# Moving the work between the stages of a graph-layer megakernel: who normalises, who zeroes, and where constants and first indices are loaded

## The chip, the cores and the metric

One core of one Trainium2 chip runs the whole program in one launch. The metric is the device time of that launch in microseconds (us), as the median of several runs. The core has five engines with a queue of instructions each: TensorE (PE; PEld is its weight load), VectorE (DVE), ScalarE (ACT), GpSimd (POOL) and SyncE (SP). ACTq, SPq and so on are an engine's queue when it only issues a transfer. Engines wait for each other by semaphores, and a code block ends with a barrier of all engines.

## The reference

The input `x` has 12500 rows of 256. There are 212500 edges, sorted by destination.

```python
xn = _layernorm(x)
x = x + gnn(xn, src, dst, edge_weight) + mix(xn)   # two GCN layers; linear attention and an MLP
x = x + ffn(_layernorm(x))                          # 8 experts, one per row
# a GCN layer:
support = x @ W
msgs = support[edge_src] * edge_weight[:, None]
agg = segment_sum(msgs, edge_dst, num_segments=N)
h = elu(agg + b)
```

What matters here is the row norm at the start, and the two GCN layers, each of which reads 212500 rows by index and adds them up by destination.

## The kernel before

The program has six stages, each a block of its own between barriers: `prepare`, `gather` for layer 1, a small block `kv`, `gather` for layer 2, routing and scattering, and the experts. The change touches the first four.

**Prepare** (from L110). It normalises `x` into the scratch tensor `xn`. One step takes a block of 256 rows (128 partitions, `PB` = 2 rows each, 256 KB); 52 blocks pass through `PSLOTS` = 4 slots. SP loads a slot as soon as its last use is normalised; VectorE takes the statistics (`bn_stats`, `bn_aggr`, L273 and L277); ScalarE the root of the variance (L211); VectorE the reciprocal (L282) and the normalisation itself (L288, two instructions of 256 columns); ScalarE's queue stores the slot (L204). VectorE runs one slot ahead: statistics of slot s, then the rest of slot s-1. Before its first block VectorE reduces the destinations of the edges to windows (L254 to L267), GpSimd sends the result through memory and back (L237 to L246), and after the last block VectorE makes the tables of relative destinations (L307 to L333). SP then loads eleven constants (L197: weights and biases of later stages, and the edge weights `wgt`), and VectorE scales three of them (L335 to L337). The block ends when all of it is done.

**Gather** (from L342), once per layer. The edges go in 104 turns of 2048. In a turn GpSimd issues 16 indirect DMAs (L451), each of which fetches 128 rows by index, into one of two buffers (u = 0 and 1). VectorE builds 16 selection matrices `sel` from destinations and weights (`take`, L460 to L403), TensorE multiplies rows by selections into `sums` (L395), and VectorE adds four windows into the table `agg` (L409). Beside that each turn carries a tile of other work: keys and values of the attention in layer 1 (`keys_values`), the attention with its MLP in layer 2 (`attend`, from L1019 on VectorE), and the dense product of an earlier tile (`dense_first`, `dense_second`).

The order of the work around the change is that of the code: each engine runs its own list, and waits where a semaphore is named. GpSimd begins a turn when the turn's indices have landed (`idx_loaded`) and when TensorE has started its products on the other buffer (`rows_used`). TensorE gives buffer 0 free at its start and buffer 1 with its first product, so in each layer GpSimd can issue 16 DMAs ahead of TensorE and no more. A turn's products also wait for the windows of the turn before (`turn_added`). At the head of each gather VectorE zeroes `agg` (128 x 25216, L467), then runs `dve_begin` of the two other parts, then `take(0, 0)`. SP loads the first two turns' indices at the head of each gather (L415). Block `kv` (L821 to L830) copies the sums of layer 1's attention out of PSUM after the first gather.

Of the kernel before, what the change touches and what calls it, by code (L numbers as in the profile page):

```python
# [5 lines left out]
F32 = mybir.dt.float32  # L6
I32 = mybir.dt.int32
# [39 lines left out]
PSLOTS = 4  # L47
# [11 lines left out]
assert 1 << LOG_WIN == WIN and 1 << LOG_TB == TB and NP >= N and TURNS % 2 == 0 and NT % (PB * PSLOTS) == 0  # L59
# [50 lines left out]
def prepare(nc, m):  # L110

    with ExitStack() as ctx:
        def sb(name, shape, dt):
# [9 lines left out]
        rstd = sb("ln_rstd", [P, PSLOTS, PB], F32)  # L123
        dst_rows = sb("dst_rows", [TURNS, TURN, GROUP * P], I32)
# [18 lines left out]
        consts_loaded = sem("consts_loaded")  # L143
# [8 lines left out]
        step = sem("prepare_step")  # L152
        spans_done = sem("spans_done")
# [9 lines left out]
        x_blocks = m.x.rearrange("(b p j) f -> b p j f", p=P, j=PB)  # L163
        xn_blocks = m.xn[0:NP, :].rearrange("(b p j) f -> b p j f", p=P, j=PB)
        n_blocks = NT // PB
        loops = n_blocks // PSLOTS
        consts = [
            (m.w_q[:, :, :], m.in_w_q.rearrange("(k p) n -> p k n", p=P)),
            (m.w_m[:, :, :], m.in_w_m.rearrange("(k p) n -> p k n", p=P)),
            (m.w_1[:, :, :], m.in_w_1.rearrange("(k p) n -> p k n", p=P)),  # L170
            (m.w_2[:, :, :], m.in_w_2.rearrange("(k p) n -> p k n", p=P)),
            (m.ln1_gh[:, :], m.in_ln1_g),
            (m.ln1_b[:, :], m.in_ln1_b),
            (m.ln2_gh[:, :], m.in_ln2_g.rearrange("(o n) -> o n", o=1).to_broadcast([P, D])),
            (m.ln2_b[:, :], m.in_ln2_b.rearrange("(o n) -> o n", o=1).to_broadcast([P, D])),
            (m.gate_w[:, :, :], m.in_gate_w.rearrange("(k p) n -> p k n", p=P)),
            (m.gate_b[:, :], m.in_gate_b.rearrange("(o n) -> o n", o=1).to_broadcast([P, NE])),
            (m.wgt[:, 0:NCH], m.in_wgt),
        ]

        with nc.Block("prepare") as block:
            @block.sync
            def _(sp):
# [12 lines left out]
                for to, of in consts:  # L196
                    sp.dma_start(to, of).then_inc(consts_loaded, 16)  # L197
                sp.wait_ge(consts_loaded, 16 * len(consts))

            @block.scalar  # L200
            def _(act):
                def store(i, s):
# [4 lines left out]
                act.wait_ge(eps_set, 1)  # L207
                with act.Fori(0, loops) as i:
                    for s in range(PSLOTS):
# [3 lines left out]
                        if s:  # L213
                            store(i, s - 1)
                    store(i, PSLOTS - 1)
                act.wait_ge(zero_set, 1)

                act.dma_start(m.xn[NP:NP + P, :], m.zeros[:, 0:D]).then_inc(pad_stored, 16)
# [5 lines left out]
            def _(pool):  # L224
                nc.gpsimd.memset(m.zeros[:, :], 0.0).then_inc(zero_set, 1)
# [21 lines left out]
                             m.more_dram.rearrange("(o t) g -> o t g", o=1)).then_inc(spans_back, 16)  # L247

            @block.vector
            def _(dve):  # L250
                nc.vector.memset(m.eps[:, :], LN_EPS).then_inc(eps_set, 1)
                dve.wait_ge(edges_loaded, 32)
# [15 lines left out]
                stat_steps = 7  # L268

                def statistics(i, s):  # L270
                    dve.wait_ge(x_loaded[s], 16 * i + 16)
                    for j in range(PB):
                        last = nc.vector.bn_stats(stats[:, s, j, :], rows[:, s, j, :])  # L273
                    last.then_inc(step, 1)
                    wait_apart(dve, step, i * PSLOTS + (s + stat_steps), m.passed)
                    for j in range(PB):
                        last = nc.vector.bn_aggr(mv[:, s, j, :], stats[:, s, j, :])  # L277
                    last.then_inc(mv_done, 1)

                def normalise(i, s, first):  # L280
                    dve.wait_ge(sd_done, i * PSLOTS + (s + 1))
                    nc.vector.reciprocal(rstd[:, s, :], sd[:, s, :]).then_inc(rstd_done, 1)  # L282
                    dve.wait_ge(rstd_done, i * PSLOTS + (s + 1))
                    if not first:

                        dve.wait_ge(xn_stored[s], 16 * i)
                    for j in range(PB):
                        last = nc.vector.tensor_scalar(normed[:, s, j, :], rows[:, s, j, :], mv[:, s, j, 0:1],  # L288
                                                       rstd[:, s, j:j + 1], ALU.subtract, ALU.mult)
                    last.then_inc(xn_done, 1)  # L290

                def turn(i, first):

                    for s in range(PSLOTS):
                        statistics(i, s)
                        if s:
                            normalise(i, s - 1, first)
                        elif not first:
                            normalise(i - 1, PSLOTS - 1, isinstance(i, int) and i == 1)
# [1702 lines left out]
```

## Time and profile before

| | |
|---|---|
| median of 3 runs | 5263.27 us (5253.92 to 5268.12) |
| the profiled execution | 5257.51 us |
| its span | 5255.6 us |
| mean granted TensorE clock | 0.85 of 2.4 GHz |
| PE, DVE, ACT, POOL busy | 4074.3, 2650.4, 814.5, 3445.0 us |

The span runs from the first to the last instruction of the profiled execution; 1.9 us of its time lie outside. The stages take about 148 us (prepare), 2126 us (first gather with `kv`), 2150 us (second gather) and 830 us (the rest). A busy time on GpSimd here is the making of a DMA's descriptors.

### The profile page before, as it was taken

What the parts mean: (1) busy time and instruction counts of PE and PEld (TensorE: products, weight loads), DVE (VectorE), ACT (ScalarE), POOL (GpSimd) and SP (SyncE); (2) the same over time, 40 slices, a digit from 0 to 9 for tenths busy, and PEclk for the clock granted to TensorE, in tenths of its full rate; (3) what the DMA queues carried; (4) which work ended last, traced back from release to release, by engine and by line L of the source; (5) the groups of instructions that cost most, each with busy time, mean ns of one, the idle gap of its engine ahead of it and who ended that gap; (6) DMA issues with size and microseconds to landing.
All of it is one profiled execution on the core that took longest, in us unless ns stands there. A gap on an engine that the chain in (4) does not pass through costs nothing. (4 is left out here: it accounts for less than half of the span.)

```text
span 5255.6 us, 89454 instructions
## 1 busy us (share of the span) xinstructions
PE 4074.3 (78%) x25266; PEld 3747.3 (71%) x25267; DVE 2650.4 (50%) x9578; ACT 814.5 (15%) x2507; POOL 3445.0 (66%) x3639
## 2 busy tenths in 40 slices
PE   0577777777777777769988999898989987069998
PEld 0467666666667776758888888888888886058886
DVE  7433333333333333355676666767666666234444
ACT  2001111111111111111222222222222222011111
POOL 0577777777777777757777777777777774632222
PEclk9867777777777777778999999999999998589999
DMA  7444444444444444434555454555545553632221
GB/s 212 142 128 132 130 132 132 130 132 130 132 131 133 132 130 132 129 89 125 147 147 152 143 151 145 147 149 146 151 144 148 147 146 109 188 112 70 67 70 65
DMA packets 409075, 693.81 MB, mean 132 GB/s; under 512 B 108237, under 2 KB 275661, under 8 KB 408893
## 3 DMA queue, kind: packets, MB, share of 16 engines
q0 software_dynamic: 177312, 488.43, 32.8%
q1 hardware_dynamic: 195765, 163.17, 10.6%
q10 hardware_dynamic: 35920, 41.25, 2.2%
q8 instruction: 40, 0.66, 0.0%
q14 instruction: 38, 0.31, 0.0%
HBM read 562.84 MB, written 129.68 MB: 132 GB/s over the span
## 5 line engine op out<-in xcount | busy, mean ns | idle before, releaser
L395 PEld LDWEIGHTS sums<-sel,rows 128*128 128x128 f32 x13312 | 1888.7, 222 | 768.0 <-DMA rows<-xn,idx 440.8
L395 PE MATMUL sums<-sel,rows 128*128 128x64 f32 x13312 | 1894.5, 305 | 672.9 <-DMA rows<-xn,idx 354.6
L451 POOL DMA_INDIRECT rows<-xn,idx x1664 | 1577.8, 948 | 642.4 <-issue 630.8
L451 POOL DMA_INDIRECT rows<-h,idx x1664 | 1585.3, 953 | 578.5 <-issue 528.9
L403 DVE TENSOR_SCALAR sel<-cols,rel_now,wgt_now 128x64 f32<-128x64 f32 x3360 | 780.4, 336 | 7.8
L409 DVE TENSOR_TENSOR agg<-agg,sums 128x128 f32 x832 | 240.3, 289 | 783.9 <-issue 604.7
L603 DVE TENSOR_TENSOR pre<-z,b_g 128x256 f32<-128x256 f32 x98 | 41.6, 424 | 526.8 <-PE z L598 526.8
L1807 PE MATMUL y_ps<-w,e_hidden 128*128 128x256 f32 x1248 | 286.1, 389 | 0.0
L1795 PE MATMUL e_hidden_ps<-tokens_t,w 128*128 128x256 f32 x1248 | 279.2, 381 | 4.4 <-DVE e_hidden L1864 3.6
L983 PE MATMUL hidden_ps<-xt,w 128*128 128x128 f32 x1664 | 265.2, 282 | 17.2 <-ACT msg_t L1104 17.0
L1735 POOL DMA_INDIRECT out<-y_result,target_i x80 | 79.5, 994 | 291.3 <-DVE y_result L1849 271.3
L1795 PEld LDWEIGHTS e_hidden_ps<-tokens_t,w 128*128 128x128 f32 x1248 | 237.5, 191 | 40.0 <-DVE e_hidden L1864 6.6
L1807 PEld LDWEIGHTS y_ps<-w,e_hidden 128*128 128x128 f32 x1248 | 241.8, 196 | 33.3
L983 PE MATMUL hidden_ps<-msg_t,w 128*128 128x128 f32 x1664 | 254.2, 275 | 0.0
L983 PEld LDWEIGHTS hidden_ps<-xt,w 128*128 128x128 f32 x1664 | 221.3, 193 | 35.3 <-ACT msg_t L1104 35.3
L946 PE MATMUL row_ps<-w,hidden 128*128 128x256 f32 x832 | 223.6, 418 | 2.7 <-ACT hidden L1108 2.7
L983 PEld LDWEIGHTS hidden_ps<-msg_t,w 128*128 128x128 f32 x1664 | 219.7, 192 | 0.0
L779 PE MATMUL kv_proj<-w_k,kv_xt 128*128 128x256 f32 x416 | 210.0, 660 | 0.0
L795 DVE TENSOR_SCALAR k_min<-kv_proj 128x256 f32<-128x256 f32 x104 | 44.1, 424 | 302.3 <-PE kv_proj L779 302.3
L946 PEld LDWEIGHTS row_ps<-w,hidden 128*128 128x128 f32 x832 | 170.1, 215 | 26.1 <-ACT hidden L1108 2.9
L971 PE MATMUL row_ps<-w_m,msg_t 128*128 128x256 f32 x416 | 125.4, 426 | 71.2 <-ACT msg_t L1096 71.2
L779 PE MATMUL kv_proj<-w_v,kv_xt 128*128 128x256 f32 x416 | 174.8, 567 | 0.0
(211 smaller groups left out, 4547.4 us busy)
## 6 DMA issues: line engine op xcount, KB each, us to landing
xe<-zeros ACTq DMA_DIRECT2D x104, 258.0 KB, 4.1
rows<-xn,idx POOLq DMA_INDIRECT x1664
rows<-h,idx POOLq DMA_INDIRECT x1664
w<-in_ffn_w POOLq DMA_DIRECT2D x16, 1024.0 KB
tile<-xn SPq DMA_DIRECT2D x105, 128.0 KB
ln_rows<-in_x SPq DMA_DIRECT2D x52, 256.0 KB
xn<-ln_normed ACTq DMA_DIRECT2D x52, 256.0 KB, 4.4
kv_tile<-xn SPq DMA_DIRECT2D x104, 128.0 KB
```

The lines of the kernel that those rows point to most:

```text
L395: last = nc.tensor.matmul(sums[:, g, h, :], rows[:, u, k, h * P:(h + 1) * P], sel[:, u, k, :], start=(c == 0), stop=(c == GROUP - 1))
L403: last = nc.vector.tensor_scalar(sel[:, u, k, :], m.cols[:, :], rel_now[:, u, k:k + 1], wgt_now[:, u, k:k + 1], ALU.is_equal, ALU.mult)
L409: return nc.vector.tensor_tensor(window, window, sums[:, g, :, :], ALU.add)
L451: nc.gpsimd.indirect_dma_start(out=rows[:, u, k, :], out_offset=None, in_=source, in_offset=bass.IndirectOffsetOnAxis(ap=idx[:, u, k:k + 1 ...
L779: last = nc.tensor.matmul(proj[n][:, 0, :], xt[:, k, :], w[:, k, :], start=(k == 0), stop=(k == KD - 1))
L795: nc.vector.tensor_scalar(k_min[:, :], proj[0][:, 0, :], 0.0, None, ALU.min).then_inc(k_min_ready, 1)
L946: last = nc.tensor.matmul(row_ps[1], hidden[:, o, :], m.w_2[:, o, :], start=(o == 0), stop=(o == F1 // P - 1))
L971: last = nc.tensor.matmul(row_ps[0], msg_t[:, k, :], m.w_m[:, k, :], start=(k == 0), stop=(k == KD - 1))
L983: last = nc.tensor.matmul(hidden_ps[:, o, :], m.w_1[:, k, o * P:(o + 1) * P], of, start=(k == 0), stop=(k == 2 * KD - 1))
L1735: nc.gpsimd.indirect_dma_start(out=m.out, out_offset=bass.IndirectOffsetOnAxis(ap=target_i[:, tt:tt + 1], axis=0), in_=result[:, tt, :], i ...
L1795: last = nc.tensor.matmul(hidden_ps[f % HB], w1[u][:, k, f * P:(f + 1) * P], tokens_t[:, k, :], start=(k == 0), stop=(k == KD - 1))
L1807: last = nc.tensor.matmul(y_ps[tt], hidden[:, f, tt * P:(tt + 1) * P], w2[u][:, f, :], start=(f == 0), stop=(f == FC - 1))
```

## The change

- **The norm.** ScalarE does the normalisation, as one activation per 256 columns with the reciprocal as scale and a shift as bias; VectorE computes the shift (minus mean times reciprocal). Seven slots in place of four, 49 blocks in place of 52: the six tiles of padding past row 12543 are zeroed by one store, issued by ScalarE's queue at the start. ScalarE's table for root and identity is loaded once, ahead of the loop.
- **Edge tables.** VectorE takes the first seven blocks' statistics before the reductions over the edges, and makes the tables before the last seven blocks rather than after them.
- **Constants.** `wgt` is loaded by GpSimd's queue at the start. The ten other constants are loaded by SP at the head of the first gather, behind its own two weights and ahead of the dense part's; VectorE scales three of them at the end of the first gather.
- **Indices.** The buffer `idx` is shared by both gathers. SP loads the first two turns' indices at the end of prepare for the first gather, and at the end of the first gather for the second. GpSimd's first two turns are written out ahead of its loop.
- **Zeroing.** For layer 1 GpSimd zeroes `agg` in prepare, after its last transfer there. For layer 2 VectorE still does, but after `take(0, 0)`.
- **`kv`** is no block of its own; its copies stand at the end of VectorE's list in the first gather (`dve_close`).

```diff
-PSLOTS = 4
+PSLOTS = 7
...
-        n_blocks = NT // PB
+        n_blocks = UNITS // PB
...
-                for to, of in consts:
-                    sp.dma_start(to, of).then_inc(consts_loaded, 16)
-                sp.wait_ge(consts_loaded, 16 * len(consts))
+                for u in range(2):
+                    sp.dma_start(m.idx[:, u, :], m.in_src[u]).then_inc(m.idx_first, 16)
+                sp.wait_ge(m.idx_first, 32)
...
+                def normalise(i, s, first):
+                    wait_apart(act, rstd_done, 2 * (i * PSLOTS + s + 1), m.act_passed)
+                    if not first:
+                        act.wait_ge(xn_stored[s], 16 * i)
+                    for j in range(PB):
+                        last = nc.scalar.activation(normed[:, s, j, :], rows[:, s, j, :], ACT.Identity,
+                                                    scale=rstd[:, s, j:j + 1], bias=shift[:, s, j:j + 1])
+                    last.then_inc(xn_done, 1)
                     act.wait_ge(xn_done, i * PSLOTS + s + 1)
...
+                act.preload_act_table_set("sqrt_and_others")
...
+                pool.dma_start(m.wgt[:, 0:NCH], m.in_wgt).then_inc(wgt_loaded, 16)
                 nc.gpsimd.memset(m.zeros[:, :], 0.0).then_inc(zero_set, 1)
...
+                nc.gpsimd.memset(m.agg[:, :, :], 0.0).then_inc(agg_zeroed, 1)
...
+                def scale(i, s):
+                    dve.wait_ge(sd_done, i * PSLOTS + (s + 1))
+                    nc.vector.reciprocal(rstd[:, s, :], sd[:, s, :]).then_inc(rstd_done, 1)
+                    dve.wait_ge(rstd_done, 2 * (i * PSLOTS + s) + 1)
+                    nc.vector.scalar_tensor_tensor(shift[:, s, :], mv[:, s, :, 0], -1.0, rstd[:, s, :],
+                                                   ALU.mult, ALU.mult).then_inc(rstd_done, 1)
...
+                turn(0, True)
                 dve.wait_ge(edges_loaded, 32)
...
-                turn(0, True)
-                turn(1, False)
-                with dve.Fori(2, loops) as i:
+                with dve.Fori(1, loops - 1) as i:
                     turn(i, False)
-                normalise(loops - 1, PSLOTS - 1, False)
...
+                turn(loops - 1, False)
+                scale(loops - 1, PSLOTS - 1)
+                wait_apart(dve, agg_zeroed, 1, m.passed)
...
                 for u in range(2):
-                    sp.dma_start(idx[:, u, :], m.in_src[u]).then_inc(idx_loaded[u], 16)
                     mix.load(sp, u, u)
                 mix.load_weights(sp)
                 dense.load_weights(sp)
...
+                if layer == 1:
+                    for u in range(2):
+                        sp.wait_ge(rows_loaded[u][BANKS - 1], 16 * GROUP * SUB * loops)
+                        sp.dma_start(idx[:, u, :], m.in_src[u]).then_inc(m.idx_first, 16)
...
+                pool.wait_ge(m.idx_first, 32 * layer)
+                turn(0)
+                wait_apart(pool, rows_used[1], 1, m.pool_passed)
+                turn(1)
+                with pool.Fori(1, loops) as i:
...
-                nc.vector.memset(m.agg[:, :, :], 0.0).then_inc(agg_zeroed, 1)
+                take(0, 0)
+                if layer == 2:
+                    nc.vector.memset(m.agg[:, :, :], 0.0).then_inc(agg_zeroed, 1)
                 mix.dve_begin(dve)
                 dense.dve_begin(dve)
-                take(0, 0)
...
+        for to, of in consts:
+            sp.dma_start(to, of).then_inc(consts_loaded, 16)
```

Three places show how the engines' lists change. The names are the program's tiles; a row is one instruction, or several of one kind.

ScalarE in prepare, one block inside the loop, before: root, then the address and the issue of the store of the slot before.

```order
L211 ACTIVATE ln_sd<-ln_mean_var,eps 128x2 [waits mean_var_done]
L204 ISA [waits xn_done]
L204 DMA xn<-ln_normed 128x512
L210 REGISTER_ALU
L211 ACTIVATE ln_sd<-ln_mean_var,eps 128x2 [waits mean_var_done]
```

The same place in the changed kernel:

```order
L206 ACTIVATE ln_sd<-ln_mean_var,eps 128x2 [waits mean_var_done]
L66 REGISTER_ALU
L194 REGISTER_ALU [waits rstd_done]
L196 ACTIVATE ln_normed<-ln_rows,ln_shift,ln_rstd 128x256 [waits xn_stored0]
L196 ACTIVATE ln_normed<-ln_rows,ln_shift,ln_rstd 128x256
L200 ISA [waits xn_done]
L200 DMA xn<-ln_normed 128x512
```

Two activations of 256 columns have moved in between the root and the store, and the store's wait is now for ScalarE's own work.

VectorE at the head of the second gather, before, from the copies of `kv` on:

```order
L830 COPY kv<-kv_total1 32x2
L821 UNCONDITIONAL_BRANCH
L456 UNCONDITIONAL_BRANCH
L467 MEMSET agg 128x25216
L1019 TENSOR_SCALAR q_min2<-tile_ps2 128x256
L1357 MEMSET logits 128x48
L460 COPY rel_now2<-dst_rel 128x16
L462 COPY wgt_now2<-wgt 128x16
L403 TENSOR_SCALAR sel2<-cols,rel_now2,wgt_now2 128x64 x16
L1041 SCALAR_TENSOR_TENSOR q_min2<-tile_ps2,q_min2 128x256
```

The same place in the changed kernel:

```order
L858 COPY kv<-kv_total1 32x2
L408 UNCONDITIONAL_BRANCH
L465 UNCONDITIONAL_BRANCH
L469 COPY rel_now2<-dst_rel 128x16
L471 COPY wgt_now2<-wgt 128x16
L400 TENSOR_SCALAR sel2<-cols,rel_now2,wgt_now2 128x64 x16
L478 MEMSET agg 128x25216
L1048 TENSOR_SCALAR q_min2<-tile_ps2 128x256
L1386 MEMSET logits 128x48
L1070 SCALAR_TENSOR_TENSOR q_min2<-tile_ps2,q_min2 128x256
```

The first selections stand ahead of the zeroing; the attention's first step (`q_min2`) still stands behind it.

GpSimd from the end of prepare into the first gather, before:

```order
L246 DMA more_row<-more_dram 1x16x13
L181 UNCONDITIONAL_BRANCH
L79 ISA
L443 UNCONDITIONAL_BRANCH
L445 UNCONDITIONAL_BRANCH
L445 ISA
L66 REGISTER_ALU
L451 DMA rows<-xn,idx 128x256 x32
```

And in the changed kernel:

```order
L250 DMA more_row<-more_dram 1x16x13
L252 MEMSET agg 128x25216
L170 UNCONDITIONAL_BRANCH
L79 ISA
L443 UNCONDITIONAL_BRANCH
L447 DMA rows<-xn,idx 128x256 x32
```

The zeroing of the table has come to GpSimd's list in prepare, and its first 32 indirect DMAs stand ahead of the loop.

## Rows read from the trace of the kernel before

**Rows 1.** The page's costliest groups, GpSimd: count | busy us, mean ns | idle before

```profile
L451 POOL DMA_INDIRECT rows<-xn,idx x1664 | 1577.8, 948 | 642.4 <-issue 630.8
L451 POOL DMA_INDIRECT rows<-h,idx x1664 | 1585.3, 953 | 578.5 <-issue 528.9
```

**Rows 2.** Timeline of the first gather: start us, us, engine, line [idle before it]

```profile
147.97 0.33 SPq L415 DMA_DIRECT2D idx<-in_src  x1
...
150.71 1.04 POOL L451 DMA_INDIRECT rows<-xn,idx  x1 [126.78 <-issue]
...
153.30 21.07 DVE L467 MEMSET agg<- 128x25216 f32 x1 [6.42 <-issue]
...
169.59 0.95 POOL L451 DMA_INDIRECT rows<-xn,idx  x1 [0.30 <-issue]
...
178.30 3.64 PE L395 MATMUL sums<-sel,rows 128*128 128x64 f32 x16 [19.42 <-DVE sel L403]
...
179.76 0.94 POOL L451 DMA_INDIRECT rows<-xn,idx  x1 [9.23 <-issue]
...
2243.12 0.95 POOL L451 DMA_INDIRECT rows<-xn,idx  x1 [0.30 <-issue]
```

**Rows 3.** Timeline of prepare: first edges, one block, tables, last wait

```profile
9.99 2.29 DVE L254 TENSOR_REDUCE low<-dst_rows 104x4 int32<-104x2048 int32 x1 [8.87 <-DMA dst_i<-in_dst]
...
16.17 0.74 DVE L273 BATCH_NORM_STATS2 ln_stats<-ln_rows 128x6 f32<-128x256 f32 x2
...
42.34 0.29 ACT L211 ACTIVATE ln_sd<-ln_mean_var,eps 128x2 f32<-128x2 f32 x1 [1.58 <-DVE ln_mean_var L277]
42.39 0.73 DVE L288 TENSOR_SCALAR ln_normed<-ln_rows,ln_mean_var,ln_rstd 128x256 f32<-128x256 f32 x2
...
43.28 0.37 ACTq L204 DMA_DIRECT2D xn<-ln_normed  x1
...
136.28 0.19 DVE L307 CAST cols<-iota_i 128x64 f32<-128x64 int32 x1
...
140.03 0.07 DVE L333 MEMSET wgt<- 128x16 f32 x1
146.31 0.17 DVE L335 TENSOR_SCALAR ln_gh<-ln_gh 128x2 f32<-128x2 f32 x1 [6.21 <-DMA wgt<-in_edge_weight]
```

**Rows 4.** Stretches of prepare: us, busy (count) by engine, PEclk, DMA share, GB/s

```profile
60.00:110.00 50.00, 0.00 (x0) 0.00 (x0) 38.33 (x154) 12.07 (x26) 0.00 (x0) 1.00 0.81 227
136.00:144.00 8.00, 0.00 (x0) 0.00 (x0) 4.01 (x16) 0.00 (x0) 0.00 (x0) 1.00 1.07 385
```

**Rows 5.** Groups by shape, ScalarE and GpSimd: count | busy us, mean ns | idle before

```profile
L1104 ACT ACTIVATE msg_t<-turn_ps,ln_b,ln_gh 128x128 f32<-128x128 f32 x208 | 84.1, 457 | 59.6 <-PE turn_ps L976 59.5
...
L1077 ACT COPY xt<-tile_ps 128x256 f32<-128x256 f32 x105 | 39.5, 376 | 3.5 <-PE tile_ps L932 3.4
...
L1819 ACT COPY tokens_t<-e_turn_ps 128x512 f32<-128x512 f32 x40 | 23.4, 586 | 241.5 <-PE e_turn_ps L1784 241.5
...
L1744 POOL MEMSET y_zeros<- 128x512 f32 x1 | 0.6, 603 | 0.0
```

**Rows 6.** Timeline between the two gathers and of the second one's start

```profile
2271.02 0.28 DVE L825 MEMSET kv<- 128x264 f32 x1 [3.90 <-PEq L411]
...
2273.74 0.36 SPq L415 DMA_DIRECT2D idx<-in_src  x1
...
2276.36 0.94 POOL L451 DMA_INDIRECT rows<-h,idx  x1 [32.30 <-DMA idx<-in_src]
...
2279.07 21.07 DVE L467 MEMSET agg<- 128x25216 f32 x1 [6.47 <-issue]
...
2300.81 3.66 DVE L403 TENSOR_SCALAR sel<-cols,rel_now,wgt_now 128x64 f32<-128x64 f32 x16
...
2306.07 0.95 POOL L451 DMA_INDIRECT rows<-h,idx  x1 [10.00 <-issue]
...
2323.84 1.90 PE L395 MATMUL sums<-sel,rows 128*128 128x64 f32 x16
```

More of the change, by code:

```diff
@@ L205, in store, with turn @@
                                   normed[:, s, :, :]).then_inc(xn_stored[s], 16)
-                act.wait_ge(eps_set, 1)
-                with act.Fori(0, loops) as i:
+                def turn(i, first):
                     for s in range(PSLOTS):
@@ L213, in _ @@
                         if s:
-                            store(i, s - 1)
-                    store(i, PSLOTS - 1)
+                            normalise(i, s - 1, first)
+                    normalise(i, PSLOTS - 1, first)
+                act.preload_act_table_set("sqrt_and_others")
                 act.wait_ge(zero_set, 1)
-                act.dma_start(m.xn[NP:NP + P, :], m.zeros[:, 0:D]).then_inc(pad_stored, 16)
+                tiles = (NP - UNITS * P) // P + 1
+                act.dma_start(m.xn[UNITS * P:NP + P, :].rearrange("(t p) f -> p t f", p=P),
+                              m.zeros[:, 0:D].rearrange("p (o f) -> p o f", o=1).to_broadcast([P, tiles, D])
+                              ).then_inc(pad_stored, 16)
+                act.wait_ge(eps_set, 1)
+                turn(0, True)
+                with act.Fori(1, loops) as i:
+                    turn(i, False)
                 act.wait_ge(pad_stored, 16)
@@ L251, in _, with statistics, turn @@
                 nc.vector.memset(m.eps[:, :], LN_EPS).then_inc(eps_set, 1)
+                def statistics(i, s):
+                    dve.wait_ge(x_loaded[s], 16 * i + 16)
+                    for j in range(PB):
+                        last = nc.vector.bn_stats(stats[:, s, j, :], rows[:, s, j, :])
+                    last.then_inc(stats_done, 1)
+                    wait_apart(dve, stats_done, i * PSLOTS + s + 1, m.passed)
+                    for j in range(PB):
+                        last = nc.vector.bn_aggr(mv[:, s, j, :], stats[:, s, j, :])
+                    last.then_inc(mv_done, 1)
+                def scale(i, s):
[4 more added lines that the diff above has]
+                                                   ALU.mult, ALU.mult).then_inc(rstd_done, 1)
+                def turn(i, first):
+                    for s in range(PSLOTS):
+                        statistics(i, s)
+                        if s:
+                            scale(i, s - 1)
+                        elif not first:
+                            scale(i - 1, PSLOTS - 1)
+                turn(0, True)
                 dve.wait_ge(edges_loaded, 32)
@@ L564, in _ @@
                 dense.pe_end(pe)
-        mix.after()
 def dense_first(nc, m, sb, sem, ps, shared):
@@ L1117, in attend @@
     mix.load_weights = lambda sp: None
-    mix.after = lambda: None
+    mix.dve_close = lambda dve: None
     return mix
```

130 lines of the change are left out of this document (56 added, 74 removed).

## The prediction

> **What bounds the kernel now.** I read the page's groups first. The two gathers issue 1664 indirect DMAs each, and GpSimd is busy 0.95 us with one [rows 1]. The timeline of the first gather then shows what stands between two of them: from the DMA at 179.76 to the last at 2243.12 there are 1647 steps in 2063.4 us, 1.253 us each, with 0.30 us of idle time at every step [rows 2]. So from its seventeenth DMA on the first gather is nothing but GpSimd's issue rate: 16 x 1.253 = 20.05 us a turn, whatever TensorE and VectorE do. The second gather has the same step (0.95 us busy each [rows 1]) with a few gaps more. A change that leaves that rate alone can gain only at the seams: the time before GpSimd's first DMA of each gather, and the time in which it stands still near the head. I looked for these next.
>
> There are four. Prepare keeps GpSimd from its first DMA until 150.71. After 16 DMAs it stands 10.17 us instead of 1.25 (169.59 to 179.76), because buffer 1 is given free by TensorE's first product, which starts at 178.30, waiting for selections that VectorE makes behind 21.07 us of zeroing [rows 2]. Between the gathers, block `kv` starts at 2271.02, the next block's first instruction is at 2273.74, and GpSimd's first DMA at 2276.36 waited for its indices [rows 6]. At the head of the second gather it stands still again, 10.00 us until 2306.07, behind the same zeroing [rows 6].
>
> Prepare itself isn't held by transfers: in its loop the DMA engines moved 227 GB/s, and 385 GB/s in the stretch behind it [rows 4]. From 16.17 to 136.28 it takes 52 blocks, 2.31 us each [rows 3]; VectorE is busy 38.33 of 50 us [rows 4], or 1.77 us a block, and waits on ScalarE for the rest.
>
> **Part 1, prepare's pace.** VectorE loses the two normalising instructions (0.73 us [rows 3]) and gains a shift of 2 columns (about 0.15, an estimate like the other tiny ones): 1.77 - 0.73 + 0.15 = 1.2 busy, with its semaphore gaps some 1.4 us a block. ScalarE gains what VectorE loses. A pair of its activations with scale and bias read per partition takes 84.1 / 104 = 0.81 us at 128 columns, and 256 columns more cost 586 - 376 = 210 ns, so 128 more cost 0.105 [rows 5]: 0.81 + 2 x 0.105 = 1.02 us for a block. Its list for a block is then the root 0.29, the pair 1.02, 0.16 from the end of normalising (42.39 + 0.73) to the store's issue at 43.28, the issue 0.37 [rows 3], and 0.1 of register work (an estimate): **1.94 us**. That is more than VectorE's 1.4 and more than the 1.4 us that 2 x 262 KB take at 385 GB/s, so ScalarE becomes prepare's bound. Bounds of its pace: 1.4 (VectorE's, if the pieces overlap), and 2.3 (two activations that don't overlap, 2 x 0.56, and 0.3 of registers).
>
> The first block. Its load stands behind the two edge loads in SP's queue, which landed at 9.99 [rows 3]; 0.26 MB more at 385 GB/s is 0.7. New in the same moments are `wgt` (0.85 MB) and the store of padding (0.92 MB), 4.6 us at that rate if all of it goes first. So the block lands between 10.7 and 15.3; I take 14, since three queues share. Its root starts 1.2 later, the second block's 1.4 behind it, and those up to the sixth at 1.94: 14 + 1.2 + 1.4 + 4 x 1.94 = 24.4. VectorE scales the sixth (0.7) and turns to the edge reductions, 16.17 - 9.99 = 6.2 us [rows 3]. ScalarE's seventh normalisation waits for them and for the statistics and scaling behind them (1.6), since VectorE runs only one block ahead: 32.9, and 1.55 for the pair and its store: 34.4. Six rounds of seven blocks follow, 6 x (7 x 1.94 + 0.3 for the branch) = 83.3: 117.7. The tables ahead of the last round take 140.10 - 136.28 = 3.8 [rows 3], of which two normalisations hide about 1.8: 119.7. The last store lands some 4 us later: 123.7. The block's closing takes 1.1 (from the end of the scalings begun at 146.31 to 147.97 [rows 2, 3]): the first gather starts at **124.8 instead of 147.97, 23.2 earlier**. The 6.21 us wait for the last constant [rows 3] is gone with it. The new loads of indices are hidden by the last stores. GpSimd's zeroing is priced at nothing because it has from about 40 us to 120 and takes between 21.07 (VectorE's time for it [rows 2]) and 25216 / 512 x 0.603 = 29.7 us [rows 5]; without that cover it would cost its length (rival B).
>
> **Part 2, the first gather's head.** GpSimd now starts 150.71 - 147.97 = 2.74 after the block [rows 2]. With its indices there this is between 0.3 (its idle time between two DMAs) and 2.74; I take 0.9, a gain of 1.8. The zeroing is off VectorE, which starts 5.33 us into the block (153.30 - 147.97 [rows 2]) and makes its selections in some 4 us. TensorE also waits for the dense part's weights, which SP now issues behind ten constants: 9 us of issue, landing near 15 us into the block (estimate; 25 at worst). GpSimd needs buffer 1 at 0.9 + 20.05 = 21: no stall, and 10.17 - 1.25 = **8.9 us** gained, 5 at worst. The 2.3 MB of constants share the DMA engines with the rows; the gather's stretch has room. Every later turn keeps its 20.05 us.
>
> **Part 3, between the gathers.** The copies of `kv` now run on VectorE while SP still waits for its last store, so the block's 2273.74 - 2271.02 = 2.7 us shrinks to a closing of 0.7: **2.0** gained (0.5 to 2.7). The three scalings join them there. SP's loads of indices now stand ahead of its last stores of `h` and wait for the last rows; those stores have some 10 us of room.
>
> **Part 4, the second gather's head.** Here the zeroing stays on VectorE, behind the selections instead of ahead of them, and the stall moves rather than goes. TensorE's first product no longer waits, so GpSimd runs 32 DMAs through, to 0.9 + 40.1 = 41 us into the block. But it then wants buffer 0, which TensorE frees with turn 1's first product, and that needs turn 0's windows, hence the attention's steps behind the zeroing. Before: zeroing ended 26.4 into the block (2279.07 + 21.07 - 2273.74), turn 1's product came 23.7 later, at 2323.84, and GpSimd began turn 2 at 2306.07 + 20.05, 52.4 into the block [rows 6]. After: VectorE's first instruction again at 5.33, selections 4.0 (3.66 and two copies [rows 6]), zeroing to 30.4. Of the 23.7, the selections' 4.0 go, and about 2 of products made earlier: 18, so 48.4. GpSimd follows 1.46 behind the product (179.76 - 178.30 [rows 2]): turn 2 at 49.9, **2.5** sooner than 52.4, with a new wait of some 9 us at the thirty-third DMA. Bounds: 0 (nothing of the 23.7 goes but what the later zeroing takes) to 11.4 (no stall, 41).
>
> **Sum.** 23.2 + 1.8 + 8.9 + 2.0 + 2.5 = 38.4. Everything behind the second gather's head is shifted, not changed. Against the profiled execution's 5257.5 that gives 5219.1. The median of the three runs lies 5.8 above that execution, the mean of all four 3.2; I put the forecast at **5220**.
>
> **Rivals.**
> - **B, GpSimd's zeroing holds VectorE up.** Both write the same memory, and if one of the loop's VectorE instructions can't run beside the long GpSimd one, VectorE stops for up to 21 to 30 us, and ScalarE one block later: about 22 lost, **5242**. For it: no row shows a long GpSimd instruction beside VectorE's loop. Against: the selections run beside GpSimd's issues in 3.66 us [rows 6]. The Trainium skill, SBUF — State Buffer, section Who interferes with whom, says that a GpSimd instruction holds a port pair it shares with VectorE for its whole length, and that VectorE's copies, casts and tensor_scalars stop for it, others with two SBUF inputs only if GpSimd reads. By that the statistics and the shift run on, while the reciprocal is in neither list; no run here shows it.
> - **C, the second head's stall goes altogether.** VectorE's first instruction comes 5.33 us into both gathers though it waits for nothing [rows 2, 6]. If the new code takes that away, zeroing ends at 25 and turn 2 can start near 44.6: 5.3 more, **5215**; with less behind the zeroing, 5211. The Trainium skill, Runtime: NRT & Kernel Launch, section Instruction fetch mechanics, says that a branch out of the fetched window costs a fetch before the engine goes on; by that the lag depends on where the new code falls. The trace agrees in that the lag is the same twice.
> - **D, ScalarE's pieces overlap** and VectorE bounds prepare at 1.43: 48 x 0.51 = 24 more, **5195**. Against: the store's issue waits for its own normalisation.
> - **E, slower: ScalarE is too slow for the norm.** Each 0.1 us a block costs 4.8 us, so from 1.94 + 38.4 / 48 = 2.74 us a block on the change loses. At 3.3, as with one table load more a block, it gives **5284**. Against: the order shows one load ahead of the loop, and the bound from rows is 2.3.
>
> **How the numbers follow.** Forecast 0.70, B 0.08, C 0.11, D 0.08, E 0.03. The low end takes in D, 5195; the high end takes the pace of 2.3 (48 x 0.36 = 17) with the late first block, and B: 5243. A measurement of this kernel can tell about 0.3%, 15.8 us, from no change. Faster by more than that needs 23 of the 38 us to hold: 0.93. E is slower, 0.02 of it by over 0.3%; the rest is within.
>
> **What would show it.** Right: ScalarE's stores in prepare 1.9 to 2.0 us apart and no table load in the loop; GpSimd's first DMA near 126; no gap at its seventeenth DMA of either gather, and one of about 9 us at the second gather's thirty-third; 1.253 us a step in between. Wrong: stores 2.3 us or more apart; a hole in VectorE's statistics while GpSimd zeroes; a gap at the seventeenth DMA (weights behind constants); another step than 1.253, since 1% of it is 42 us in the two gathers, more than all I count.

## The result, and the profile after

The changed kernel takes 5373.92 us (median of four runs, 5364.52 to 5380.38) against 5259.25 before (5253.92 to 5268.12): a ratio of **1.0215, 95% interval 1.0193 to 1.0237**. It is slower by 2.1%, where the prediction said 5220. The profiled execution spans 5374.1 us, against 5255.6 before.

GpSimd's issues cut the span into five stretches, each of which can be set against its counterpart. These are the rows of the changed kernel's timeline for them (start us, us, engine, line [idle before it]); the rows of before are [rows 2, 6].

```profile
124.04 1.04 POOL L447 DMA_INDIRECT rows<-xn,idx  x1 [67.98 <-POOLq L80]
...
146.96 0.94 POOL L447 DMA_INDIRECT rows<-xn,idx  x1 [3.05 <-PE sums L392]
...
2214.06 0.95 POOL L447 DMA_INDIRECT rows<-xn,idx  x1 [0.30 <-issue]
...
2243.22 0.95 POOL L447 DMA_INDIRECT rows<-h,idx  x1 [28.21 <-POOLq L80]
...
2296.87 0.94 POOL L447 DMA_INDIRECT rows<-h,idx  x1 [13.89 <-PE sums L392]
...
4520.52 0.95 POOL L447 DMA_INDIRECT rows<-h,idx  x1 [0.30 <-issue]
```

Of before, one row more is needed, the last DMA of its second gather:

```profile
4406.95 0.95 POOL L451 DMA_INDIRECT rows<-h,idx  x1 [0.30 <-issue]
```

| stretch, us | before | after | difference |
|---|---|---|---|
| start to GpSimd's first DMA | 150.7 | 124.0 | -26.7 |
| first gather, first to last DMA | 2092.4 | 2090.0 | -2.4 |
| last DMA to the second gather's first | 33.2 | 29.2 | -4.1 |
| second gather, first to last DMA | 2130.6 | 2277.3 | **+146.7** |
| last DMA to the end of the span | 848.7 | 853.6 | +4.9 |

So by the second gather's first DMA the change is 33.1 us ahead, and everything is lost in that gather. GpSimd's own step is the same there (1.25 us between most of its DMAs, 0.30 idle), but from about 2600 us on it stands still in nearly every turn, for 0.8 to 5.3 us. Two of these places:

```profile
2691.04 0.94 POOL L447 DMA_INDIRECT rows<-h,idx  x1 [5.28 <-issue]
...
2755.59 0.94 POOL L447 DMA_INDIRECT rows<-h,idx  x1 [2.75 <-PE sums L392]
```

The engine that makes it wait is found in the groups of VectorE's instructions: `q_min` in line 1070 (1041 before) is the first instruction that works behind the loop's jump. First how its idle time is split in the kernel before (us, times), then in the changed one:

```profile
L1041 DVE SCALAR_TENSOR_TENSOR q_min<-tile_ps,q_min x104: 409/425/426, 2304.4 to 4405.9; 128x256 f32<-128x256 f32 x104
its engine sat idle before it (us, times) until:
  ACT q_min L1081: 49.6, 103
```

```profile
L1070 DVE SCALAR_TENSOR_TENSOR q_min<-tile_ps,q_min x104: 423/425/426, 2273.9 to 4520.8; 128x256 f32<-128x256 f32 x104
its engine sat idle before it (us, times) until:
  issue: 150.4, 45
  ACT q_min L1110: 28.5, 59
```

"issue" is idle time in which the engine waited for nothing that the profile shows. It comes 45 times, 3.3 us each. The loop has 46 rounds of two turns, so that is once at each jump back: VectorE stands still right behind it. The 150.4 us are about what the gather loses, 146.7. What moved meanwhile is in the page's section on DMA queues (packets, MB, share of 16 engines), before and after:

```profile
q14 instruction: 38, 0.31, 0.0%
```

```profile
q14 instruction: 265, 2.17, 0.1%
```

The 227 packets more are five for each of 45 jumps (225) and two besides, and 2.17 MB / 265 is 8192 bytes a packet. Their start times in the trace fit: in each of the 45 stops two of these packets begin, the first within 1.2 us of the stop's start. So at each jump back VectorE's instructions are fetched again. No instruction of the loop was changed; what changed is where it stands, because other VectorE instructions ahead of it were added.

The Trainium skill, Runtime: NRT & Kernel Launch, section Instruction fetch mechanics, says that a taken branch whose target isn't in the fetched window forces a fetch before the engine goes on. The trace agrees, at 3.3 us a time.

### The profile page after: what moved, and what is told of

It reads as the page before. It is cut to its first block and busy times, and to the rows that moved or that the text cites. A ratio compares the mean times of both kernels' runs of the same rounds, so it can differ in the third digit from the quotient of the medians.

```text
span 5374.1 us, 89394 instructions
## 1 busy us (share of the span) xinstructions
PE 4167.9 (78%) x25266; PEld 3824.0 (71%) x25267; DVE 2601.0 (48%) x9507; ACT 851.0 (16%) x2590; POOL 3472.7 (65%) x3641
## 3 DMA queue, kind: packets, MB, share of 16 engines
q14 instruction: 265, 2.17, 0.1%
## 5 line engine op out<-in xcount | busy, mean ns | idle before, releaser
L392 PEld LDWEIGHTS sums<-sel,rows 128*128 128x128 f32 x13312 | 1919.7, 225 | 743.5 <-DMA rows<-xn,idx 441.3
L392 PE MATMUL sums<-sel,rows 128*128 128x64 f32 x13312 | 1922.5, 308 | 646.8 <-DMA rows<-xn,idx 352.0
L1012 PE MATMUL hidden_ps<-xt,w 128*128 128x128 f32 x1664 | 266.7, 283 | 13.9 <-ACT msg_t L1133 13.6
L975 PE MATMUL row_ps<-w,hidden 128*128 128x256 f32 x832 | 256.8, 464 | 3.1 <-ACT hidden L1137 3.1
L975 PEld LDWEIGHTS row_ps<-w,hidden 128*128 128x128 f32 x832 | 191.3, 241 | 33.4 <-ACT hidden L1137 3.3
L1042 ACT ACTIVATE ln_var<-var 128x1 f32<-128x1 f32 x208 | 42.2, 203 | 880.7 <-DVE var L1024 880.7
L1813 PE MATMUL e_turn_ps<-ident,tokens 128*128 128x128 f32 x160 | 27.2, 298 | 189.8 <-DMA tokens<-xe 189.8
```

Source lines behind the costliest of these rows:

```text
L392: last = nc.tensor.matmul(sums[:, g, h, :], rows[:, u, k, h * P:(h + 1) * P], sel[:, u, k, :], start=(c == 0), stop=(c == GROUP - 1))
L975: last = nc.tensor.matmul(row_ps[1], hidden[:, o, :], m.w_2[:, o, :], start=(o == 0), stop=(o == F1 // P - 1))
L1012: last = nc.tensor.matmul(hidden_ps[:, o, :], m.w_1[:, k, o * P:(o + 1) * P], of, start=(k == 0), stop=(k == 2 * KD - 1))
L1042: nc.scalar.activation(ln_var[:, n, :], var[:, n, :], ACT.Ln).then_inc(log_ready[n], 1)
```

## The experiments

**The place of the loop.** Counted in the built programs, VectorE's loop of the second gather is 328 instructions long and begins at its instruction 3093 in the kernel before and 3144 in the changed one. My theory: what counts is how many pieces of 128 instructions the loop touches, one packet of 8192 bytes each. (That a packet holds 128 is at first an estimate: the same section of the Trainium skill gives 32 KiB as 512 instructions, 64 bytes each. The runs with 128 memsets below test it.) From 3093, place 21 of a piece, it ends at place 348 and touches three; from 3144, place 72, it ends at place 399 and touches four. To move it and nothing else, small memsets of a spare tile stand at VectorE's very start, in `prepare`:

```diff
                 nc.vector.memset(m.eps[:, :], LN_EPS).then_inc(eps_set, 1)
+                for k in range(77):
+                    nc.vector.memset(pad[:, k:k + 1], 0.0)
```

Four kernels, two made from the changed one and two from the kernel before:

> The changed kernel with 77 small memsets of one column each (a spare tile, never read) on VectorE at the very start of the prepare block, where VectorE otherwise waits for the first rows of x until 13.03 us (hidden: that much idle is there). They move every later VectorE instruction 77 places on, so that the loop of the second gather begins at VectorE's instruction 3221 instead of 3144, which is exactly 128 places behind its 3093 in the kernel before. Theory (place of the loop in VectorE's code): the refetch after each back-branch (44 of them at a mean of 3.46 us, 152.4 us together, against 9.2 us before) goes, the instruction packets of the queue q14 fall from 265 to some 40 to 60, and the time falls from 5374 to 5374 - 143 = 5231, with the 33.1 us that the seams gained kept: 5215 to 5235. Rival (something the edits do in the second gather itself: the sums zeroed later, the new form of the gather's loop, the early indices): no instruction of that gather changes, so 5365 to 5385 stays.

> The same with 128 small memsets. Theory (place of the loop relative to pieces of 128 instructions, 8192 bytes, the size of one packet of q14): a whole piece more leaves the loop where it stands in its pieces, so the refetches stay, 5365 to 5390, and 240 to 290 packets on q14. Rival (any shift helps, or the memsets at the start help by themselves): 5215 to 5240, as with 77.

> The kernel before, none of the edits, with 51 of the same small memsets at VectorE's start, so that its second gather's loop begins at instruction 3144, the place that it has in the changed kernel. Theory: the refetches come, some 44 x 3.2 us = 143 us and more, 5390 to 5410, and over 240 packets on q14. Rival (the edits themselves): 5250 to 5270, as the kernel before.

> The kernel before with 128 of the memsets (one whole piece of 8192 bytes). Theory: same place within its pieces, so 5255 to 5275 (VectorE has idle time at the start for most of the memsets) and about 38 packets on q14. Rival (more code ahead of the loop is what costs, wherever it then stands): 5350 or more.

And four that put the ends of the loop near a piece's edge, with one run each:

> The changed kernel with 64 of the small memsets. The second gather's loop is 328 VectorE instructions long; with 64 it runs from instruction 3208 to 3535, which is places 8 to 335 counted from a multiple of 128, within three pieces of 128. Theory (no refetch while the loop lies within three pieces): 5210 to 5240, 38 to 60 packets on q14. Rival (only the very place of the kernel before is good): 5360 to 5390.

> The changed kernel with 48 of the small memsets: the loop runs from 3192, place 120 of a piece, to 3519, so that its first 8 instructions lie in a fourth piece. Theory: the refetches are back, 5360 to 5390 and 240 packets or more on q14, although only 16 memsets fewer than with 64 stand ahead. Rival (pieces begin elsewhere than at the multiples of 128 that I count, or a loop that overhangs by a few instructions is spared): 5210 to 5240.

> The kernel before with 28 of the small memsets: its loop runs from 3121, place 49, to place 376, within three pieces (384). Theory: as the kernel before, 5245 to 5270, some 38 packets on q14. Rival (every shift of the kernel before costs): 5390 or more.

> The kernel before with 44 of the small memsets: its loop runs from place 65 to place 392, so its last 9 instructions, the back-branch among them, lie in a fourth piece. Theory: refetches, 5390 to 5420, 240 packets or more on q14. Rival (the pieces end later): 5245 to 5270.

Measured:

| kernel | memsets | loop's places | pieces | packets on q14 | us | ratio to before, 95% |
|---|---|---|---|---|---|---|
| before | 0 | 21 to 348 | 3 | 38 | 5259 | |
| b_pad28 | 28 | 49 to 376 | 3 | 38 | 5261.1 (one run) | |
| b_pad44 | 44 | 65 to 392 | 4 | 264 | 5413.2 (one run) | |
| b_pad51 | 51 | 72 to 399 | 4 | 264 | 5410.4 | 1.0283 (1.0266 to 1.0301) |
| b_pad128 | 128 | 21 to 348 | 3 | 39 | 5257.5 | 1.000 (0.999 to 1.001) |
| changed | 0 | 72 to 399 | 4 | 265 | 5373.9 | 1.0215 (1.0193 to 1.0237) |
| a_pad48 | 48 | 120 to 447 | 4 | 265 | 5496.8 (one run) | |
| a_pad64 | 64 | 8 to 335 | 3 | 40 | 5233.9 (one run) | |
| a_pad77 | 77 | 21 to 348 | 3 | 40 | **5223.1** | 0.9936 (0.9919 to 0.9954) |
| a_pad128 | 128 | 72 to 399 | 4 | 266 | 5372.4 | 1.0214 (1.0197 to 1.0231) |

All eight came out on the theory's side, and none as its rivals would have it. The kernel before, with none of the edits, is 2.8% slower when its loop stands where the changed kernel's does (b_pad51), and the changed kernel is 0.64% faster than before when its loop stands where the old one did (a_pad77). That it isn't the number of instructions ahead is told by the two with 128: a whole piece more changes nothing, in either kernel. The idle rows of `q_min` go the same way, here in a_pad77 and then in b_pad51:

```profile
  ACT q_min L1113: 50.1, 104
```

```profile
  issue: 150.1, 45
  ACT q_min L1084: 28.0, 58
```

Two pairs of neighbours tell where a piece begins: 64 memsets are fast, 48 are not, and 28 are fast ahead of the old loop and 44 are not. The fast places seen are 8, 21 and 49, the slow ones 65, 72 and 120, and of 128 places the 57 from 0 to 56 should be fast. What the engine holds beyond that isn't measured.

a_pad48 had been expected at 5360 to 5390 and took 5497: the direction held, the size didn't. Its packets are as many, but VectorE stands still at a second place in the round as well. These are its groups for `q_min` and for `rel_now`, the copy right behind it (count | busy us, mean ns | idle before):

```profile
L1073 DVE SCALAR_TENSOR_TENSOR q_min<-tile_ps,q_min 128x256 f32<-128x256 f32 x104 | 44.2, 425 | 156.7 <-issue 128.2 <-ACT q_min L1113 28.5
...
L472 DVE COPY rel_now<-dst_rel 128x16 f32 (+1 forms) x210 | 39.3, 187 | 121.4 <-issue 92.6 <-DMA b_g<-in_gnn_b 15.9 <-PEq L80 6.9
```

In the changed kernel that copy had 28.8 us of idle time and none of it by "issue". The two rows by "issue" make 220.8 of the 274 us between this run and a_pad77. So the place of the loop among the pieces changes the price too, not only whether it is paid; which instructions stand at the edges may be the reason, but that wasn't followed up.

**ScalarE normalises.** With the loop at a good place, the parts can be told apart. The first is the largest term of the prediction.

```diff
-                    wait_apart(act, rstd_done, 2 * (i * PSLOTS + s + 1), m.act_passed)
...
-                        last = nc.scalar.activation(normed[:, s, j, :], rows[:, s, j, :], ACT.Identity,
-                                                    scale=rstd[:, s, j:j + 1], bias=shift[:, s, j:j + 1])
...
                     nc.vector.reciprocal(rstd[:, s, :], sd[:, s, :]).then_inc(rstd_done, 1)
...
+                        last = nc.vector.tensor_scalar(normed[:, s, j, :], rows[:, s, j, :], mv[:, s, j, 0:1],
+                                                       rstd[:, s, j:j + 1], ALU.subtract, ALU.mult)
```

> One part undone: VectorE normalises again (root on ScalarE, reciprocal and the two subtract-and-scale instructions on VectorE, ScalarE only issues the store), all else as in the changed kernel, seven slots and edge tables beside the rows included. The second round of prepare is written out, so 114 small memsets stand ahead instead of 77, which puts the second gather's loop at instruction 3349, again place 21 of a piece. Theory (the prediction's part 1): a block goes back from some 1.92 us to some 2.3, over 42 to 48 blocks 16 to 18 us: GpSimd's first DMA near 141 instead of 124.6, and 5237 to 5243 against 5223. Rival (the seven slots and the rows that start earlier gain it, ScalarE is not needed): GpSimd's first DMA at 126 or before and 5218 to 5228.

Measured: 5241.75 us, ratio 0.9965 (0.9952 to 0.9979), GpSimd's first DMA at 143.09. The numbers are the theory's, and the theory is wrong all the same. The timeline of VectorE and GpSimd in `prepare` (one pair a block, 0.74 us) shows where the 18 us are:

```profile
37.92 0.77 DVE L271 TENSOR_SCALAR ln_normed<-ln_rows,ln_mean_var,ln_rstd 128x256 f32<-128x256 f32 x2
...
39.83 21.42 DVE L271 TENSOR_SCALAR ln_normed<-ln_rows,ln_mean_var,ln_rstd 128x256 f32<-128x256 f32 x2
...
62.38 0.74 DVE L271 TENSOR_SCALAR ln_normed<-ln_rows,ln_mean_var,ln_rstd 128x256 f32<-128x256 f32 x2
```

```profile
39.65 21.13 POOL L246 MEMSET agg<- 128x25216 f32 x1
```

One pair took 21.42 us; it began 0.18 us behind GpSimd's zeroing and ended 0.47 behind it. Nothing else in prepare is slower. The roots on ScalarE that open a round give the pace: a round of four blocks before, then one of seven in the changed kernel, then one of seven with VectorE normalising again (a77_norm_dve).

```profile
64.36 1.28 ACT L211 ACT_TABLE_LOAD   x1 [3.35 <-DVE ln_normed L288]
65.66 0.48 ACT L211 ACTIVATE ln_sd<-ln_mean_var,eps 128x2 f32<-128x2 f32 x2
...
73.65 1.28 ACT L211 ACT_TABLE_LOAD   x1 [3.46 <-DVE ln_normed L288]
74.94 0.48 ACT L211 ACTIVATE ln_sd<-ln_mean_var,eps 128x2 f32<-128x2 f32 x2
```

```profile
76.01 0.48 ACT L206 ACTIVATE ln_sd<-ln_mean_var,eps 128x2 f32<-128x2 f32 x2 [0.94 <-ACT ln_normed L196]
...
90.35 0.48 ACT L206 ACTIVATE ln_sd<-ln_mean_var,eps 128x2 f32<-128x2 f32 x2 [0.94 <-ACT ln_normed L196]
```

```profile
83.31 0.53 ACT L200 ACTIVATE ln_sd<-ln_mean_var,eps 128x2 f32<-128x2 f32 x2 [3.36 <-DVE ln_normed L271]
...
96.84 0.53 ACT L200 ACTIVATE ln_sd<-ln_mean_var,eps 128x2 f32<-128x2 f32 x2 [3.35 <-DVE ln_normed L271]
```

That is 9.28 us for four blocks (2.32 each), 14.34 for seven (2.05) and 13.53 for seven (1.93). VectorE normalising is the faster of the two, so it isn't the engine that shortened a block. The rows of before show what did: a load of ScalarE's table stands ahead of the first root of every round, and the changed kernels load it once, ahead of their loop. This is the group of the loads in before:

```profile
L211 ACT ACT_TABLE_LOAD x13 | 16.7, 1283 | 43.3 <-DVE ln_normed L288 42.1 <-DVE eps L251 1.1
```

VectorE's reciprocal has to wait for the root behind that load. This is its idle time by it (us, times) in before (L282), then in a77_norm_dve (L266):

```profile
  ACT ln_sd L211: 12.7, 12
```

```profile
  ACT ln_sd L200: 0.2, 1
```

That is 12.7 of the 20 us or so by which 52 blocks of 2.32 differ from 52 of 1.93. The rest is left for the longer round. No run changes the load or the slots alone, so this split is read from the traces and not shown by an experiment. Taking GpSimd's zeroing away should give back the 22 us. The last experiment does that and joins it with the split below:

```diff
-                nc.gpsimd.memset(m.agg[:, :, :], 0.0).then_inc(agg_zeroed, 1)
...
+                if layer == 1:
+                    nc.scalar.activation(m.agg[:, :, :], m.zeros[:, 0:1].rearrange("p (a b) -> p a b", a=1)
+                                         .to_broadcast([P, KD, AGG]), ACT.Copy).then_inc(agg_zeroed, 1)
                 mix.act_begin(act)
```

> VectorE normalises again as in a77_norm_dve (114 memsets, the second gather's loop at place 21), and GpSimd's zeroing in prepare is taken away: ScalarE zeroes the table at the start of the first gather, and one half of it in the second (the split of a77_zero_split). In a77_norm_dve one normalising pair on VectorE took 21.42 us, ending 0.47 us behind GpSimd's zeroing of 21.13, and apart from that a round of seven blocks took 13.5 us against 14.4 with ScalarE normalising. Theory (VectorE's normalising instruction stands still while GpSimd zeroes, and that alone made ScalarE's part worth 18 us): no normalising pair over 1 us, GpSimd's first DMA at 143.1 - 22.6 + 1.9 = 122 (121 to 124), and 5208 to 5216 us, no worse than the 5213 of a77_zero_split. Rival (VectorE's pace is what holds prepare, ScalarE is needed for it): GpSimd's first DMA at 135 or later and 5222 or more.

Measured: 5211.72 us, ratio **0.9904 (0.9888 to 0.9921)**, GpSimd's first DMA at 122.19, and the pair that had taken 21.42:

```profile
39.59 0.74 DVE L269 TENSOR_SCALAR ln_normed<-ln_rows,ln_mean_var,ln_rstd 128x256 f32<-128x256 f32 x2
```

So ScalarE's part is worth nothing by its pace; beside GpSimd's zeroing it is worth 18 us, because it takes the instructions off VectorE that can't run beside it. The statistics, reciprocals and shifts of the changed kernel's loop ran beside the same 21.13 us with no such stop: the longest wait among them, 2.69 us, is for ScalarE's root. The Trainium skill, SBUF — State Buffer, section Who interferes with whom, names `tensor_scalar` among the VectorE instructions that can stop for a GpSimd instruction's whole length; the trace agrees.

**The second gather's head.**

```diff
-                take(0, 0)
                 if layer == 2:
                     nc.vector.memset(m.agg[:, :, :], 0.0).then_inc(agg_zeroed, 1)
+                take(0, 0)
```

> One part undone: in the second gather the zeroing of the sums stands ahead of the first selections again; 77 memsets, the loop at the same place as with 77. With 77 GpSimd stood 13.8 us at the thirty-third DMA and not at the seventeenth; in the kernel before 10.9 at the seventeenth. Theory from those two rows: the order of the change costs 3 us here, so 5220 against 5223, a stall of 10 to 11 us at the seventeenth DMA and none at the thirty-third. Rival (the prediction's part 4, which gave the change 2.5 us at this place): 5226, and a wait at the thirty-third DMA as well.

Measured: 5230.62 us, ratio 0.9949 (0.9934 to 0.9964), which can't be told from a_pad77's 0.9936 (0.9919 to 0.9954); the two profiled spans are 5224.8 and 5224.5. The time lies above both that were expected, 5220 and 5226. The stall is at the seventeenth DMA, and only there:

```profile
2271.45 0.94 POOL L450 DMA_INDIRECT rows<-h,idx  x1 [11.39 <-PE sums L395]
```

Whether the zeroing stands ahead of the selections or behind them moves the stall by sixteen DMAs and leaves its size within 1.5 us (12.84 behind them, in a_pad77). So neither 3 us one way nor 2.5 the other is shown.

```diff
-                    nc.vector.memset(m.agg[:, :, :], 0.0).then_inc(agg_zeroed, 1)
+                    nc.vector.memset(m.agg[:, 0, :], 0.0).then_inc(agg_zeroed, 1)
...
-                    dve.wait_ge(agg_zeroed, 1)
+                    wait_apart(dve, agg_zeroed, 2, m.passed)
...
         copy_tile(act, 0, 0)
+        nc.scalar.activation(m.agg[:, 1, :], m.zeros[:, 0:1].to_broadcast([P, AGG]), ACT.Copy
+                             ).then_inc(m.agg_zeroed, 1)
         exp_query(act, 0)
```

> With 77 memsets and, in the second gather, the zeroing split: VectorE zeroes one half of the table, ScalarE the other, between its first copy of the tile and its first exponential. Theory (the stall at the thirty-third DMA is the length of the zeroing carried through turn 0's attention): both halves are done near 2256 instead of 2269, the stall falls from 13.8 to 1 to 4 us, and the time to 5210 to 5214. It tells also what the 5.12 us of idle time are that stand ahead of the zeroing on VectorE: if they are part of the zeroing, they halve to 2.6; if they belong to the instruction, 5.1 stay and the gain is some 2 us less. Rival (the attention's chain of turn 0, not the zeroing, sets the stall; or ScalarE's half holds up its own first steps): 12 us or more of stall, 5220 to 5228.

Measured: 5212.91 us, ratio 0.9915 (0.9901 to 0.9928). GpSimd has no step over 2 us at the head of this gather any more, and the gather is 2121.4 us long instead of 2133.1 in a_pad77; the intervals of the two times overlap, the 11.7 us of the trace are what the theory said. VectorE's half:

```profile
2246.57 10.56 DVE L482 MEMSET agg<- 128x12608 f32 x1 [2.50 <-DMA b_g<-in_gnn_b]
```

## Why the prediction was wrong, point by point

**The step that failed** is the sentence in its sum, "Everything behind the second gather's head is shifted, not changed". It rests on GpSimd's issue rate as the only bound, "whatever TensorE and VectorE do", so nothing was set down for what VectorE's loop costs at its new place. But the loop's place in VectorE's code is shifted with the rest, by 51 instructions, and by that it costs 3.3 us more at each jump back. 146.7 us of loss stand against 33.1 of gain. Nor had the second gather the room that was read from the first. These are 1000 us of the first gather and 1730 of the second in the kernel before (us; busy of PE, PEld, DVE, ACT and POOL; granted clock, DMA share, GB/s):

```profile
500.00:1500.00 1000.00, 747.97 (x4098) 690.39 (x4097) 353.74 (x1349) 103.39 (x300) 756.88 (x799) 0.75 0.47 131
2650.00:4380.00 1730.00, 1553.84 (x11486) 1455.04 (x11485) 1188.15 (x4477) 390.06 (x1357) 1288.54 (x1352) 0.96 0.51 148
```

TensorE, whose products wait for VectorE in every turn, is busy for 75% of the one and 90% of the other; that this is why hardly any of VectorE's stop was hidden is argued from these rows. With the loop at its old place the same edits give 5223.1 (a_pad77), against 5220 forecast. Rival C came near the cause, since it let a fetch of code depend on where the new code falls, but only for the 5 us at a block's start.

The prediction had asked to look for another step than 1.253 us. The step itself stayed; what came was a wait in nearly every turn, from a stop of VectorE in every other.

**Prepare and the first DMA: the pace right, the reason for the gain wrong.** First DMA at 124.0, forecast some 125.7; VectorE's first block at 13.03, forecast 14; a pair of activations 1.08 us, forecast 1.02; ScalarE's stores 1.92 apart inside a round, forecast 1.94. These rows are of the changed kernel (ScalarE, two blocks):

```profile
37.52 1.08 ACT L196 ACTIVATE ln_normed<-ln_rows,ln_shift,ln_rstd 128x256 f32<-128x256 f32 x2
38.76 0.36 ACTq L200 DMA_DIRECT2D xn<-ln_normed  x1
39.24 0.29 ACT L206 ACTIVATE ln_sd<-ln_mean_var,eps 128x2 f32<-128x2 f32 x1 [0.64 <-DVE ln_mean_var L265]
39.44 1.08 ACT L196 ACTIVATE ln_normed<-ln_rows,ln_shift,ln_rstd 128x256 f32<-128x256 f32 x2
40.68 0.37 ACTq L200 DMA_DIRECT2D xn<-ln_normed  x1
```

But the gain of the loop was put down to VectorE's lighter list, from 2.31 us a block [rows 3] and 38.33 busy of 50 [rows 4]. With VectorE normalising and nothing zeroed beside it, GpSimd's first DMA comes no later (122.19, norm_dve_zero_act). Before, the seam between two rounds of four cost 9.28 - 4 x 1.88 = 1.8 us, where 1.88 is the distance of two roots within a round; with seven slots, the table loaded ahead of the loop, and VectorE normalising it costs 13.53 - 7 x 1.88 = 0.4. Of the 1.8, 1.28 is the table load. The prediction read that VectorE "waits on ScalarE for the rest", but didn't ask for what: it never costed the load that goes, nor PSLOTS going from 4 to 7. What it did cost held: three blocks fewer (3 x 2.31 = 6.9 us), the constants' wait that is gone, and ScalarE as the bound at 1.92 us a block. So its time for the first DMA was no luck; wrong is why that comes sooner than before. The table load accounts for more of it than the work that was moved, which a77_norm_dve and norm_dve_zero_act show to gain nothing by itself.

**Rival B** was false for the kernel as written, and right about the hazard: undoing ScalarE's part brought out a stop of 21.4 us, at the low end of its 21 to 30. GpSimd's zeroing itself took 21.13, within the bounds.

**The first gather's head** gained 6.2 us of stall, not 8.9: 3.05 us stay (1.35 in a_pad77, so part of it varies). It is the gap that the prediction named as a sign of weights behind constants. In the changed kernel the dense part's last weight is issued behind the ten constants, 13.6 us into the gather, and VectorE waits for it:

```profile
136.86 0.47 SPq L645 DMA_DIRECT2D b_g<-in_gnn_b  x1
```

```profile
143.72 0.20 DVE L469 COPY rel_now<-dst_rel 128x16 f32<-128x16 f32 x1 [16.48 <-DMA b_g<-in_gnn_b]
```

TensorE's first product, which frees buffer 1, starts at 145.62. That it is late for the same weight is argued from those times; no run moved the constants. The gather's length fell by less than the stall (2.4 us), and by 6.6 in a_pad77.

**Between the gathers** 4.1 us were gained, 2.0 forecast.

**The second head** was forecast to gain 2.5 with a wait of some 9 us at the thirty-third DMA. The wait is there, and none at the seventeenth, but it is 13.89 against 10.00 before [rows 6]. The mechanism held, the term was mis-sized: in a_pad77, without the refetches, the second gather is 2.5 us longer than before and not shorter. Rival C's hope that VectorE's 5.33 us ahead of the zeroing vanish fell too: in the changed kernel VectorE's copies for the selections start within 0.1 us of the block's opening at 2242.55 and the selections 0.3 us behind it, and the idle time has moved along with the zeroing.

```profile
2242.88 3.81 DVE L400 TENSOR_SCALAR sel<-cols,rel_now,wgt_now 128x64 f32<-128x64 f32 x16
2251.82 21.07 DVE L478 MEMSET agg<- 128x25216 f32 x1 [5.12 <-issue]
```

With half the table it is 2.50. That fits a zeroing that really takes 26.2 us and is recorded for the last 21.07 of them; but in the half the row names a DMA as the releaser, so this stays open.

The sum of the parts, as the traces of before and a_pad77 have them: 26.1 at the start, 6.6 in the first gather, 4.3 between, -2.5 in the second, -3.5 behind it, 31.0 in all, of 38.4 forecast.

## What to carry to other kernels

An edit also moves the code behind it. Before trusting that a hot loop is merely shifted, compare the count of instruction packets on the page and the idle time by "issue" behind the loop's jump; if both have risen, put some idle instructions ahead of the loop (or take some away) and time it again before judging the edit. A part that is undone alone can give the forecast number for another reason, so look in its trace for the place where the time went. And before a gain is put down to the part that was meant to bring it, list what else the edit took out of the loop, here a table load in each round.

## What the runs showed of the hardware that was not expected

- A loop of 328 VectorE instructions is refetched at each jump back when it touches four pieces of 128 instructions, and not when it touches three: 38 to 41 packets of 8192 bytes in a run against 264 to 266, and 150 to 274 us (b_pad51 against before, a_pad48 against a_pad77). The first gather's loop, 230 instructions, touches at most three wherever it starts, and showed none of it. The Trainium skill, in the section named above, gives blocks of 256 instructions, of which the engine holds two; here the good and bad places repeat after 128, so the measurement decides.
- VectorE's `tensor_scalar` of 128x256 stopped for 21.4 us beside a GpSimd memset of 21.13, while `bn_stats`, `bn_aggr`, `reciprocal` and `scalar_tensor_tensor` ran on beside the same memset.
- ScalarE zeroes the table in the time that GpSimd takes, 21.21 us against 21.13. In the last experiment:

```profile
121.42 21.21 ACT L528 ACTIVATE agg<-zeros 128x25216 f32<-128x25216 f32 x1 [4.70 <-PEq L80]
```
